# GPS network kernel: the mixing head's up-bias product turned over, and its messages moved into the slots

## The reference, cut to what matters

```python
def _forward(x, Wq, Wk, Wv, Wo, bo, ln1_g, ln1_b, W1, b1, W2, b2, ln2_g, ln2_b):
    for i in range(DEPTH):                                   # DEPTH = 4
        h = _layernorm(x, ln1_g[i], ln1_b[i])
        x = x + _linear_attn(h, Wq[i], Wk[i], Wv[i], Wo[i], bo[i])
        h = _layernorm(x, ln2_g[i], ln2_b[i])
        x = x + (jax.nn.gelu(h @ W1[i] + b1[i], approximate=False) @ W2[i] + b2[i])
    return x
...
x = x + _L0_gnn_ref(xn, edge_index, edge_attr_2, ...) + _L0_mix_ref(xn[None], ...)[0]
```

## Time and profile before

| | |
|---|---|
| median of 3 runs | 2770.2 us (2769.07 to 2773.22) |
| the profiled execution | span 2778.4 us, 2780.2 us as a whole |
| TensorE busy | 2393.5 us (86%), x16282 |
| VectorE busy | 1829.0 us (66%), x4645 |
| ScalarE busy | 1395.4 us (50%), x3051 |
| GpSimd busy | 1252.4 us (45%), x1406 |
| granted TensorE clock, mean | 0.929 of full |

### The profile page before, as it was taken

The page is one execution under the profiler, slowest core; times in us unless marked ns, Lnnn a source line. Parts: engine busy times, 40 slices in busy tenths (PEclk is TensorE's granted clock), DMA queues, the critical chain, the costliest instruction groups (busy, mean ns, idle before and its releaser), DMA issues. The chain is left out here.

```text
span 2778.4 us, 47683 instructions
## 1 busy us (share of the span) xinstructions
PE 2393.5 (86%) x16282; PEld 2236.8 (81%) x16282; DVE 1829.0 (66%) x4645; ACT 1395.4 (50%) x3051; POOL 1252.4 (45%) x1406
## 2 busy tenths in 40 slices
PE   6888999899989998997997899656776898888898
PEld 5878998899889988986777799546676688888798
DVE  6666877677767776655776565456655766566665
ACT  4334665455546554555643344332233555555687
POOL 1413553344424542555874322336655566665100
PEclk9889999999999999998995799868888999999999
DMA  5211112111211121125333555346654266566011
GB/s 123 64 31 39 43 46 65 38 40 43 72 31 42 43 57 34 48 56 115 92 85 101 152 156 159 99 135 171 172 167 133 80 184 195 169 185 183 24 39 31
DMA packets 150452, 259.91 MB, mean 94 GB/s; under 512 B 35793, under 2 KB 96044, under 8 KB 150086
## 3 DMA queue, kind: packets, MB, share of 16 engines
q0 software_dynamic: 49632, 145.61, 19.8%
q1 hardware_dynamic: 100582, 111.25, 13.5%
HBM read 219.96 MB, written 36.82 MB: 92 GB/s over the span
## 5 line engine op out<-in xcount | busy, mean ns | idle before, releaser
L998 POOL DMA_INDIRECT gat<-table,srcT x400 | 415.5, 1039 | 366.2 <-DVE m L2900 238.3
L1156 POOL DMA_INDIRECT x_rows<-table,srcT x392 | 403.5, 1029 | 249.8 <-issue 118.6
L656 PE MATMUL pa<-w,act 128*125 128x256 f32 x2400 | 360.2, 288 | 13.8 <-DVE act L2659 12.2
L656 PE MATMUL pb<-hT,w 128*128 128x378 f32 (+1 forms) x1920 | 338.2, 312 | 12.1 <-ACT gf L2048 11.1
L656 PEld LDWEIGHTS pa<-w,act 128*125 128x125 f32 x2400 | 315.1, 188 | 18.9 <-DVE act L2659 16.8
L656 PEld LDWEIGHTS pb<-hT,w 128*128 128x128 f32 x1920 | 287.6, 190 | 16.7 <-ACT gf L2048 9.7
L2348 ACT ACTIVATE gf<-pb,bne 128x378 f32<-128x378 f32 (+1 forms) x320 | 194.0, 606 | 187.1 <-PE pb L656 117.2
L2048 ACT ACTIVATE gf<-pb,b1s 128x378 f32<-128x378 f32 (+1 forms) x320 | 165.5, 517 | 130.1 <-PE pb L656 89.8
L2659 DVE TENSOR_TENSOR act<-gf,act 128x378 fp32r<-128x378 f32 (+1 forms) x320 | 153.6, 483 | 104.5 <-ACT act L2051 76.8
L656 PE MATMUL pb<-act,fw 128*128 128x378 f32 (+1 forms) x960 | 159.7, 313 | 20.2 <-ACT gf L2348 15.5
L656 PE MATMUL pb<-xT,fw 128*128 128x378 f32 (+1 forms) x960 | 161.3, 317 | 16.0 <-ACT gf L2348 15.4
(11 more groups left out here) (534 smaller groups left out, 5717.9 us busy)
## 6 DMA issues: line engine op xcount, KB each, us to landing
e<-in_L_ffn_W_dram SPq DMA_DIRECT2D x40, 512.0 KB, 5.2
spill<-m SPq DMA_DIRECT2D x80, 170.0 KB
msg<-spill SPq DMA_DIRECT2D x40, 340.0 KB, 2.9
yslots<-yo SPq DMA_DIRECT2D x64, 128.0 KB
fraw<-in_L_ffn_W_dram SPq DMA_DIRECT2D x32, 256.0 KB
w1r<-in_L_mix_W_dram SPq DMA_DIRECT2D x7, 1024.0 KB, 4.8
gat<-table,srcT POOLq DMA_INDIRECT x400
x_rows<-table,srcT POOLq DMA_INDIRECT x392
```

The source lines that it names most:

```text
L656: mm = nc.tensor.matmul(ps, lhs(l), rhs(r), start=first and n == 0, stop=last and n == 2)
L998: pool.indirect_dma_start(out=gat[:, i % 2, c, :], out_offset=None, in_=table0, in_offset=bass.IndirectOffsetOnAxis(ap=srcT[:, i * GC + c: ...
L1156: pool.indirect_dma_start(out=x_rows[:, n % UB, c, :].bitcast(F32), out_offset=None, in_=table1, in_offset=bass.IndirectOffsetOnAxis(ap=sr ...
```

## The change

The up-bias product is turned over: two columns per block of `ln2_b` are stationary (one of them zero, so that both halves of the 1024 results land in their own row of one bank), and 512 columns of W1 move: four matmuls for 32 instructions before. The row result goes to SBUF on ScalarE (`bias_row`), to memory and back by two DMAs on SyncE's queue, the second of which turns it (element by element) into the layout of `b1t`, and VectorE adds `b1` in `mix_matrix(l)`. The product moves from the end of groups 0 to 3 to the middle of groups 1 to 4, where the ten filler products stood. All four head messages go; slots with g = 0 make four messages instead of three.

```diff
--- before.py
+++ after.py
@@ -107,9 +107,9 @@
 KW = D + 1
 PAIRS = ((0, 2), (2, 1), (3, 2))
 RING = (0, 1, 2, 0, 1)
-MSG_HEAD = 4
+MSG_HEAD = 0
 MSG_RING = 4
-MSG_SLOT = (3, 4, 4, 4, 4)
+MSG_SLOT = (4, 4, 4, 4, 4)
 BR = 3 * GT * NE
 UC = 2
 UG = RR
@@ -173,6 +173,7 @@
     table1 = dram("table1", (N, 2 * D))
     table2 = dram("table2", (N, D))
     yslots = dram("yslots", (NUN * UT, D))
+    b1_rows = dram("b1_rows", (NL, FF))
     spill = dram("spill", (NCG, P, CG * MW))
 
 
@@ -344,6 +345,9 @@
     minus = sb("minus", [P, TP], R32, s5)
     two_rows = sb("two_rows", [P, 1], F32, s5)
     quarter = sb("quarter", [1, P], F32, s5)
+    lnbz = sb("lnbz", [P, NL, H, 2, 2], F32, s5)
+    b1row = sb("b1row", [2, 2, FF // 2], F32, s5)
+    b1t = sb("b1t", [P, NL, FT], F32, s5)
     wv = sb("wv", [P, H, D], F32, s5)
     wo = sb("wo", [P, H, D], F32, s5)
     kmx = sb("kmx", [TP, D], F32, s5)
@@ -611,7 +615,7 @@
         s[n] = sem(n)
 
     past = {}
-    for new, old, value in (("e_ld0", "wq_ld", 128), ("e_ld1", "bo_ld", 128), ("e_ld2", "wvo_ld", 128), ("e_ld3", "sm_ld", 320),
+    for new, old, value in (("e_ld0", "wq_ld", 128), ("e_ld1", "bo_ld", 128), ("e_ld2", "wvo_ld", 128), ("e_ld3", "sm_ld", 320 + 32 * NL),
                             ("row2_st0", "row_st", 32 * NG + 16), ("row2_st1", "x_ld", 32), ("x_ld1", "p7_ld", 0), ("x_ld2", "p9_ld", 0),
                             ("x_ld3", "f_ld0", 0), ("x_ld4", "f_ld1", 0), ("be6_ld", "w_ld", 48),
                             ("z_add", "tn_T", NL), ("z_ve", "cx_ps", NL), ("z_nr", "cx_go", NL), ("hot_w", "bq_ps", NL), ("b1_go", "bq_ev", NL), ("deg_used", "mo_ps", NL), ("lgt_ps", "km_red", NL * NG), ("lgt_go", "mo_hi", NL), ("us_hi", "bq_go", NL), ("us_lo", "km_go", NL * NG),
@@ -822,11 +826,16 @@
                          m2[:, i % 2].rearrange("p c f -> p (c f)")).then_inc(s[f"msg_st{i % 2}"], 16)
 
         down_load(0)
-        for i in range(MSG_HEAD):
-            if i + 1 < NL:
-                sp.wait_ge(s["b1_ps"], i + 1)
-                bias_load(NL - 2 - i)
-            store_message(i)
+        for i in range(NL):
+            l = NL - 1 - i
+            sp.wait_ge(s["b1_ps"], i + 1)
+            if l:
+                bias_load(l - 1)
+            sp.wait_ge(s["b1_ready"], i + 1)
+            sp.dma_start(b1_rows[l].rearrange("(r c) -> r c", r=2), b1row[:, i % 2, :]).then_inc(s["sm_ld"], 16)
+            sp.wait_ge(s["sm_ld"], 16 * 5 * NL + 32 * i + 16)
+            sp.dma_start(b1t[:, l, :], b1_rows[l].rearrange("(f p) -> p f", p=P),
+                         allow_slow_non_contiguous=True).then_inc(s["sm_ld"], 16)
         for k, (l, g) in enumerate(slots):
             if g == 0 and l + 1 < NL:
                 sp.wait_ge(s["qp_ps"], 3 * NG * (l + 1))
@@ -1033,8 +1042,6 @@
             if g + 1 < NG:
                 for part in range(2):
                     n_root(0, g + 1, part)
-            if g:
-                fetch_next(g - 1)
         for l in range(NL):
             more = l + 1 < NL
             if l:
@@ -1435,13 +1442,13 @@
 
             pe.wait_ge(s["sm_ld"], 16 * 5 * NL)
             pe.wait_ge(s["w1b"], 16 * (NL - l))
-            to = u_ring[1].take(pe)
-            for f in range(FT):
+            to = u_ring[0].take(pe)
+            for r in range(2):
                 for h in range(H):
-                    last = nc.tensor.matmul(to[:, f:f + 1], w1r[:, h, f * P:(f + 1) * P], lnb[:, l, 1, h:h + 1],
-                                            start=h == 0, stop=h == H - 1)
+                    last = nc.tensor.matmul(to[0:2, :], lnbz[:, l, h, r, :], w1r[:, h, r * (FF // 2):(r + 1) * (FF // 2)],
+                                            start=r == 0 and h == 0, stop=r == 1 and h == H - 1)
             last.then_inc(s["b1_ps"], 1)
-            u_ring[1].used = (s["b1_ready"], NL - l)
+            u_ring[0].used = (s["b1_ready"], NL - l)
 
         def mix_up(l, g, n):
             G, u, f = group(l, g), n // FT, n % FT
@@ -1533,13 +1540,11 @@
                 spread_max(0, g - 1, u_ring[1])
             turn_n(0, g, 2)
             if g:
-                keep_warm(10)
+                up_bias(NL - g)
                 for h in range(H):
                     sum_context(0, g - 1, h)
             k_product(0, g, 2, d_ring[2])
             q_product(0, g, 2, head_q[2])
-            if g < NL:
-                up_bias(NL - 1 - g)
         for p in range(3):
             turn_q(0, 0, p)
         for l in range(NL):
@@ -2177,6 +2182,13 @@
                 if n == 14 and more:
                     k_evict(l + 1, g, 1, d_banks[spare(l, g)])
 
+        def bias_row(i):
+
+            act.wait_ge(s["b1_ps"], i + 1)
+            if i >= 2:
+                act.wait_ge(s["sm_ld"], 16 * 5 * NL + 32 * (i - 2) + 16)
+            nc.scalar.activation(b1row[:, i % 2, :], u_banks[0][0:2, :], ACT.Copy).then_inc(s["b1_ready"], 1)
+
         qk_upper(0)
         for part in range(2):
             n_apply(0, 0, part)
@@ -2189,6 +2201,7 @@
             if g:
                 k_exps(0, g - 1)
                 q_exps(0, g - 1)
+                bias_row(g - 1)
             k_evict(0, g, 2, HEAD_K[2])
             if g + 1 < NG:
                 for part in range(2):
@@ -2834,6 +2847,7 @@
             me.link(dve, nc.vector.reciprocal(cr[:, :], cs[:, :, D]))
             nc.vector.tensor_tensor(tn[:, :, :], cs[:, :, 0:D], cr[:, :].unsqueeze(2).to_broadcast([P, H, D]), ALU.mult).then_inc(s["tn_go"], 1)
             dve.wait_ge(s["tn_T"], l + 1)
+            up_bias(l)
             for f in range(H):
                 me(nc.vector.tensor_scalar(ta[:, f, :], t_bank[:, f * D:(f + 1) * D], lng[:, l, 0, f:f + 1], lnb[:, l, 0, f:f + 1], ALU.mult, ALU.add))
             me.join(dve)
@@ -2876,8 +2890,8 @@
 
         def up_bias(l):
 
-            dve.wait_ge(s["b1_ps"], NL - l)
-            nc.vector.tensor_tensor(b1s[:, l, :], bias_bank()[:, 0:FT], b1c[:, l, :], ALU.add).then_inc(s["b1_ready"], 1)
+            dve.wait_ge(s["sm_ld"], 16 * 5 * NL + 32 * (NL - l))
+            me(nc.vector.tensor_tensor(b1s[:, l, :], b1t[:, l, :], b1c[:, l, :], ALU.add))
 
         def down_bias(l):
 
@@ -2993,7 +3007,7 @@
                     h_lower(l, g + 1, 1)
                 if n == 11 and late:
                     k_subtract(l + 1, g - 1, d_banks[spare(l, g)])
-                if n == 12 and MSG_SLOT[g] > 3:
+                if n == 12:
                     message(first + 3)
                 if n == 12 and l and g == 0:
                     q_sum(l, NG - 1)
@@ -3011,6 +3025,10 @@
         me(nc.vector.tensor_scalar(minus[:, :], ones[:, 0:TP], two_rows[:, 0:1], -1.0, ALU.mult, ALU.mult))
         me(nc.vector.tensor_scalar(b2x[:, :, :].rearrange("p k (h c) -> p (k h) c", h=H), ident[:, :].unsqueeze(1).to_broadcast([P, 2 * H, P]), 0.0, None, ALU.mult))
         me.join(dve)
+        dve.wait_ge(s["sm_ld"], 16 * 5 * NL)
+        me.link(dve, nc.vector.tensor_scalar(lnbz[:, :, :, :, :].rearrange("p l h r c -> p (l h r c)"), ones[:, 0:NL * H * 4], 0.0, None, ALU.mult))
+        for r in range(2):
+            me(nc.vector.tensor_copy(lnbz[:, :, :, r, r], lnb[:, :, 1, :]))
         q_bias(0)
         for part in range(2):
             n_stats(0, 0, part)
@@ -3032,14 +3050,11 @@
                 for part in range(2):
                     n_stats(0, g + 1, part)
             if g:
-                message(g - 1)
                 for h in range(H):
                     keep_context(0, g - 1, h)
             k_max_early(0, g)
             k_max(0, g)
             q_evict(0, g, 2, HEAD_Q[2])
-            if g < NL:
-                up_bias(NL - 1 - g)
             if g in (2, 3):
                 q_sum(0, g - 2)
                 q_scale(0, g - 2)
```

## The result

The changed kernel took 2754.32 us (median of 4 runs, 2751.31 to 2759.03), the kernel before 2770.3 us beside it (4 runs, 2769.07 to 2773.22). The ratio is 0.994, with a 95% interval of 0.9918 to 0.9962: 16 us less, where 5.8 us less was forecast. The profiled execution took 2759.03 us as a whole, with a span of 2757.4 us.

A forecast was written before the change was run, and what follows sets the result against it. TensorE was taken to bound head and slots, with the product at a group's end on the head's path. Head -8.9, addition +0.5, messages +3.6, clock -1.0 gave -5.8 us from 2770.2: 2764.4 us, range 2758 to 2770.

The forecast's parts named there:

- Start of stage 2, +0.4 us: Head: three small VectorE operations ahead of `q_bias` delay everyone by 0.4 us, bounds 0.3 and 0.6.
- The product leaves the ends of groups 0 to 3: Head: removing 32 instructions, 3.5 us, brings the next `turn_max` earlier by 1.9, 3.7, 3.25 and 3.25 us.
- The product in the fillers' place, 3.4 to 3.6 us, `sum_context` 0.8 us later: Middle of groups 1 to 4: the new product replaces ten fillers of 2.40 us, costing 3.2 us in all.
- The clock, -1.0 us: Head groups 3 and 4: part of the half-clock loss returns, -1.0 us; bounds a 5.2 us gain and a 2.6 us loss.
- The rival with a full clock in groups 3 and 4: Head: the product no longer starves the array, 4.2 us more gain than forecast, 2760.2 us; chance 0.18.
- The turn by way of memory, 0: SyncE's queue: layer 0's bias is back near 188 us, before `mix_matrix(0)` asks at about 200, so cost 0.
- The addition, +0.5 us: `mix_matrix`: VectorE's addition stands on the path behind its wait for TensorE, 0.09 to 0.17 us in four layers.
- The messages, +3.6 us: Slots (l, 0): a fourth message costs 0 in (0, 0), 0.9 to 1.0 in (1, 0) and (2, 0), 1.6 in (3, 0).
- the rival, four messages at their whole price: Slots take back the gain: four messages cost 1.6 us each, 6.4, and the clock gives nothing; 2768.2 us, chance 0.13.
- The sum, -5.8 us: Head, addition, messages and clock: -8.9 + 0.5 + 3.6 - 1.0 us, set against the median.
- a head whose chain hides the gain: Head: another link sets the groups' length, half the head's gain is missing; 2769.8 us, chance 0.08.
- the half clock at the new product: Head: groups 1 and 2 fall to 1.2 GHz and the product runs at half rate, +18.8 us, 2783 us; chance 0.07.

The follow-up runs named there:

- cols_mid: Kernel before with its one-column product moved to where the ten fillers stood, in bank 0, and VectorE's addition with it: 2657.94 us, ratio 1.0022.
- rows_end: Changed kernel with messages back in the head, the new product at the ends of groups 0 to 3 and the ten fillers back: 2641.0 us, ratio 0.9963.
- quarter: Changed kernel with one of the product's four matmuls, so the up bias isn't computed in full: 2754.42 us, ratio 0.997.
- after_4b: Second of two repeats of the unchanged changed kernel on one more chip like the first; whole profiled run 2756.09 us, head 132.23 us.
- bias_only: Changed kernel with the four messages back in the head and three instead of four in slots (l, 0): 2646.64 us, ratio 0.9973.
- bias_fill: Changed kernel with messages back in the head and 16 instead of six fillers ahead of `turn_max` in groups 3 and 4: 2645.66 us, ratio 0.9971.
- msgs_only: Kernel before with only the four head messages moved to the slots: 2656.77 us, ratio 1.0023.
- sets 1 and 2: Two sets of follow-up runs, each on one chip with the kernel before beside it, there at 2651.68 and 2651.97 us.
- the first pair: The first profiled executions of the kernel before and the changed kernel: 2780.2 and 2759.03 us as a whole.
- after_4a: First of two repeats of the unchanged changed kernel on one more chip like the first; whole profiled run 2756.45 us, head 135.84 us.
- before_again: Kernel before as a copy, run against itself on a chip where it takes 2652 us: 2654.4 us, ratio 1.0004.

## Why the prediction was wrong, point by point

*Start of stage 2, +0.4 us:* right. The first operation of `q_bias` moved from 0.85 to 1.22 us behind the start of the stage.

*The product leaves the ends of groups 0 to 3.* Measured from the stage's start, `turn_max` of groups 1 to 4 is earlier by 1.3, 4.0, 6.6 and 10.3 us, where 1.9, 4.8, 7.25 and 9.7 was forecast. `sum_context` of group 1 is earlier by 0.3 (forecast 1.1), and the head's end by 9.4 (8.9, and 9.9 with the clock). The sum was good, the steps along it up to 0.8 us too high early on and 0.6 too low later. That it came within 0.5 us is in part luck: the head takes 141.55 to 145.01 us in four profiles of before and 132.23 to 136.21 in five of the changed kernel, 8.6 us less in the mean and 6.4 on the second chip.

*The reason given for it* was half wrong. I priced the product as a thing that stands on the path, and argued that it helps to take it off. `cols_mid` and `rows_end` show that the new place isn't what helps, and isn't needed: the form, with the eviction on ScalarE that comes with it, gives the whole gain. The mistake was in what I read into the earlier trace rows: the product and its slow followers (2.69 us for 12 fillers, half-clock products in groups 3 and 4) were told as two facts, length and clock, and only the first was removed in the sum. They are one: behind every one-column product the clock fell. The forecast had half of it, as the six fillers at full rate are in its sum.

*The product in the fillers' place, 3.4 to 3.6 us, `sum_context` 0.8 us later:* 3.60 us, and by `quarter` 1.0 us on the path. The bank and `bias_row` cost nothing, as forecast.

*The clock, -1.0 us:* too small. From `turn_max` to `k_subtract`, groups 3 and 4 took 9.0 and 8.9 us before, 7.7 and 7.7 after (134.93 to 142.59), so 2.5 us came back where at most 5.2 could. An idle time stayed, as forecast, and most of the rest goes with it (15 falls in 18 places, none in 6 without it). The rival with a full clock in groups 3 and 4 was therefore half true in the changed kernel, and wholly so in group 3 of `after_4b` and `bias_only`.
By the Trainium skill ("TensorE: Matmul & The Clock Gate", section "Why this matters for your kernels") a gap between bursts costs the clock. The traces agree in the main, 2.36 us of k product behind 2.66 us idle in the changed kernel against 1.66 us behind 0.43 in `bias_fill`; but 1.65 us behind the same 2.66 in `bias_only`. That the gain would be 0 by this rule, as I set beside the sum, was wrong, since clock was also lost behind the product itself.

*The turn by way of memory, 0:* right. The last turned load was issued at 172.8 us, and at 198.27 nobody waited for it. How long it took isn't shown.

*The addition, +0.5 us:* right as far as it can be read (0.08 to 0.17 us a layer).

*The messages, +3.6 us:* the waits came as forecast in slots (1, 0), (2, 0) and (3, 0), and the size was low: +6.1 us by `msgs_only` (2.4 to 9.8 by its interval). On the chips of sets 1 and 2 the slots took 1038.68 to 1042.21 us in five kernels with three messages in (l, 0) and 1045.17 and 1047.55 with four, 5.8 us more in the mean. This is nearer to the 6.4 us of the rival, four messages at their whole price. Where the part beyond the forecast comes from stays open. In the first pair the slots showed nothing of it; by the last table the slots of one kernel differ by 3.4 us from one execution to the next, which is as much as was looked for.

*The sum, -5.8 us:* three later comparisons gave -4.2, -5.3 and -6.6 us. The first gave -16.

*What failed is the range*, 2758 to 2770, and in it one step: "the sum is a difference of 123 + 1066 us of it, and I set it against the median". That gave the other 1500 us a width of nothing, and took the spread of three runs (4 us) for that of the kernel. What the runs showed in its place: behind the slots one kernel differs by 8.0 us from one execution to the next, and ahead of stage 2 by 6. Two things on the table spoke against it: the profiled execution was 10.0 us over the median, and the page put 4% of its chain to an unknown queue, which I had not read. With 22 and 19 runs the kernel before spreads over 20 and 31 us. My estimate from these, made after the fact: a range for four runs against three should have been wider by some 5 us to each side, and would have held the time. What made the four runs 16 us shorter than the three stays open: scatter alone, or with it a gain behind the slots that has no known cause.

The rivals: a head whose chain hides the gain did not come, nor did the half clock at the new product; in the changed kernel the clock was 1.00 through the product and behind it. Of the slots that take back the gain the price came nearly (5.8 to 6.1 of 6.4 us), but not the other half, a clock that gives nothing.

## What to carry to other kernels

On TensorE ask of each step not only how long it is but what clock it leaves to the next: here a one-column product and a 512-column one were both 3.6 us, and only the first was followed by a lower clock; in `cols_mid` the context sums behind it took 1.6 and 2.2 us longer. So test form and place apart: here the new form, left at the old place and with the messages left in the head, had the lowest ratio on two chips (0.9963 and 0.9948). And before giving a range, look for waits that the page can't put down to the program; where there are any, a difference of 10 us between two profiles of 2770 us is no finding.

## What the runs showed of the hardware

The same program takes 2652 us in two sets of runs, on two chips, and 2764 to 2770 us in the three others. Of the difference 98 to 108 us lies behind the slots (1395 against 1493 to 1503 us) and 9 to 17 in them (1042 against 1051 to 1060). In the longer ones ScalarE, VectorE and GpSimd wait for something outside the program, up to 15.6 us at a time: in all three profiles of before for 14.5 to 15.6 us at the same eviction of ScalarE, near 2130 us. In the eight profiles on the two chips of 2652 us no wait has such a releaser. In the ten others these waits add up to 171 to 239 us over all engines.

A product whose weight loads are busy throughout and whose moving side is one column wide (32 instructions in 3.63 us) is followed by a granted clock of 0.61 in the next 3 us, though TensorE counted as busy for the whole stretch before it at a clock of 1.00. The same result with two stationary columns and 512 moving ones (8 instructions in 3.60 us) is followed by 1.00, and so is a quarter of it (2 instructions in 1.02 us, then 1.50 us idle).

Whether the clock falls at one place of one kernel changes from execution to execution: behind the same 2.66 us idle the same k product took 1.66 us in `after_4b` and 2.84 in `after_4a`. It moves the head of one kernel by 3.6 us, and a first slow stretch that ends at 46 to 50 us, or not before stage 2, moves the whole by 6. TensorE was busy without a pause in that stretch: 10.00 of 10.00 us from 50 to 60 in `before_again`.
